# One kernel of cross attention and feed-forward: y's rows and integers in buffers of their own, half a landing buffer for the context, batch 0's K and the last tile's h by quarters

## The reference, cut to what matters

```python
def dyn_quant(x):                       # per row
    s = max(max(|x|) / 127, 1e-8);  return clip(round(x / s), -127, 127), s

x_n   = layernorm(x)
q     = w8a8(x_n, wq, bq)               # integers of x_n times integers of wq, times both scales
k, v  = ctx @ wk.T + bk, ctx @ wv.T + bv            # full precision
p     = softmax(q k^T / sqrt(32) + mask)            # 16 heads, 112 x 375
x     = x + w8a8(p v, wo, bo)
x_n   = layernorm(x)
h     = gelu(int8_matmul(rowwise(x_n), W1) + B1)    # W1, W2: one scale for the whole matrix
x     = x + int8_matmul(rowwise(h), W2) + B2
```

## Time and profile before

| | us |
|---|---|
| median of three executions | 663.83 |
| the three | 659.75, 665.29, 663.83 |
| the profiled execution | 658.58 |
| its span (first to last instruction) | 656.4 |
| PE busy | 638.5 (97%) |
| DVE busy | 474.1 (72%) |
| ACT busy | 461.1 (70%) |
| POOL busy | 223.6 (34%) |
| granted PE clock | 1.00 |

### The profile page before, as it was taken

One profiled execution on the slowest core, in us unless ns is written; L12 is line 12 of the kernel. 1 busy time (PEld: TensorE's weight loads), 2 busy tenths in 40 slices (PEclk: granted clock), 3 DMA queues, 4 the chain that ended last, 5 costly groups with the idle time before them and its releaser, 6 DMA issues.

```text
span 656.4 us, 15000 instructions
## 1 busy us (share of the span) xinstructions
PE 638.5 (97%) x5204; PEld 470.9 (72%) x5204; DVE 474.1 (72%) x1175; ACT 461.1 (70%) x1156; POOL 223.6 (34%) x455
## 2 busy tenths in 40 slices
PE   8898999999999999999999989999999999999999
PEld 4667787777777777768777777877777786767534
DVE  4989788767676766876775834775688768777874
ACT  3545676777887667787687867786777778879702
POOL 3343343252527153530525243341444252321100
DMA  9965865523252443413214253217145231413020
...
DMA packets 80586, 58.68 MB, mean 89 GB/s; under 512 B 57984, under 2 KB 67968, under 8 KB 79872
## 3 DMA queue, kind: packets, MB, share of 16 engines
...
## 4 chain that ended last, share of the span: by engine, by line
PE 75%; DVE 11%; DMA 5%; issue 4%; POOL 3%; ACT 2%; ACTq 0%; DVEq 0%; SPq 0%; POOLq 0%
PE ps_ring L1070 32%; PE ps_t L1104 12%; PE ps_s L1097 7%; PE ps_ring L1176 7%; PE ps_t L1116 6%; PE ps_ring L1189 6%; PE ps_ring L1138 2%; PE ps_ring L1063 1%; DMA w_q<-in_w1T 1%; PE ps_s L1165 1%; DVE cols L843 1%; PE ps_ring L1126 1%; DMA yqT<-o_q 1%; DMA x_in<-in_x 1%; DVE probs L872 1%
## 5 line engine op out<-in xcount | busy, mean ns | idle before, releaser
L872 DVE CUSTOM_DVE_ANT_0 probs<-ps_s,mask_in 112x375 f32<-112x375 f32 x256 | 129.6, 544 | 67.8 <-PE ps_s L1097 54.9
L690 ACT ACTIVATE probs<-probs,neg_max 112x375 f32<-112x375 f32 x256 | 154.5, 607 | 27.1 <-DVE neg_max L872 24.6
L700 ACT ACTIVATE pT<-ps_t 125x336 f32<-125x336 f32 x256 | 109.8, 446 | 70.6 <-PE ps_t L1104 64.7
L1104 PEld LDWEIGHTS ps_t<-ident,probs 112*125 112x125 f32 x768 | 107.9, 188 | 42.3 <-issue 18.6
L1104 PE MATMUL ps_t<-ident,probs 112*125 112x112 f32 x768 | 119.9, 278 | 5.6 <-ACT oT L707 2.4
L609 POOL TENSOR_TENSOR ctx_lo<-ctx_in,ctx_hi 128x376 fp32r<-128x376 f32 x60 | 63.8, 1071 | 124.7 <-ACT ctx_hi L668 124.6
L1070 PE MATMUL ps_ring<-ctx_hi,wk_hi 128*128 128x376 f32 x256 | 90.7, 354 | 1.2 <-DVE wk_lo L765 0.7
L1070 PE MATMUL ps_ring<-ctx_hi,wk_lo 128*128 128x376 f32 x256 | 85.5, 334 | 0.0
L1070 PE MATMUL ps_ring<-ctx_lo,wk_hi 128*128 128x376 f32 x256 | 85.4, 334 | 0.0
L1070 PE MATMUL ps_ring<-wv_hi,ctx_hi 128*125 128x512 f32 x192 | 79.1, 412 | 2.0 <-DVE o L882 1.0
L1070 PE MATMUL ps_ring<-wv_lo,ctx_hi 128*125 128x512 f32 x192 | 75.8, 395 | 0.0
...
## 6 DMA issues: line engine op xcount, KB each, us to landing
...
w_q<-in_w1T SPq DMA_DIRECT2D x2, 1024.0 KB, 11.3
```

The lines of the kernel that those rows point to most:

```text
L690: nc.scalar.activation(probs[:, hd % SP_RING, :], probs[:, hd % SP_RING, :], ACT.Exp, scale=-1.0, bias=neg_max[:, b % 2, hd:hd + 1], accum ...
L700: nc.scalar.activation(pT[0:LR, hd % PT_RING, :], att_bank("T", b, hd)[0:LR, 0:LC * N], ACT.Copy).then_inc(pT_s, 1)
L872: nc.vector.tensor_tensor_reduce(out=probs[:, hd % SP_RING, :], in0=ps_s[hd % HG][0:N, 0:L], in1=mask_in[:, b % 2, :], scale=-1.0, scalar= ...
L1104: last = nc.tensor.transpose(bank[0:LR, lc * N:(lc + 1) * N], probs[:, hd % SP_RING, lc * LR:(lc + 1) * LR], ident[0:N, 0:N])
```

## The change

Seven things, in the words of the code:

1. `yn` and `y_q` are buffers of their own beside `o` and `o_q`. `gather`'s row on DVE waits for `o_quant` of the tile before instead of `y_quant`; `o_quant` and `y_quant` wait each for their own transpose of the tile before.
2. `ctx_in` has two blocks instead of four and one semaphore; each half load waits until the half before it is split on both engines.
3. All `ctx_lo` subtractions are DVE's; POOL's are gone.
4. Batch 0's K goes by quarters of the contraction (`k0` units, `k_first`): a quarter adds its three products to all four K blocks, which stand in the four banks `ps_s`, and waits only for its half of wk and its block of context.
5. The last tile's h is quantised by quarters of 512 columns: DVE takes 0, 1 and 2, ACT takes 3. PE transposes each quarter into a bank of `ps_s` or `ps_t`, DVE copies 0 and 2, ACT 3 and 1, and `down` takes the quarters in the order 0, 3, 1, 2, each as it comes.
6. 13 `warm` units stand at the start, 19 at the end, and none after the last `down`.
7. All five tables of orders are new.

The diff, without the tables, without the new semaphores' declarations and without most unchanged lines:

```diff
-             if use[0] in ("w_T", "so", "w_max", "q", "k", "v", "gather", "o_T", "out_proj", "y_T", "up", "h_T") or use[0] == "down" and use[2] == 0]
+             if use[0] in ("w_T", "so", "w_max", "q", "k", "v", "gather", "o_T", "out_proj", "y_T", "up") or use[0] == "down" and use[2] == 0]
...
-        ctx_in = sb("ctx_in", [P, KC, LP])
+        ctx_in = sb("ctx_in", [P, KC // 2, LP])
...
-        o = yn = sb("o", [P, C])
-        o_q = sb("o_q", [P, C], BF16)
+        o, yn = sb("o", [P, C]), sb("yn", [P, C])
+        o_q, y_q = sb("o_q", [P, C], BF16), sb("y_q", [P, C], BF16)
...
-                sp.dma_start(yqT[:, :, :], o_q[:], transpose=True).then_inc(yqT_s, 16)
+                sp.dma_start(yqT[:, :, :], y_q[:], transpose=True).then_inc(yqT_s, 16)
...
-            def split_lo(b, i):
-                if b == 1 and i == 0:
-                    pool.wait_ge(ctx_lo_s, 4)
-                pool.wait_ge(ctx_hi_s, 4 * b + i + 1)
-                wait_for(pool, k_pe, 4 * (b - 1))
-                wait_for(pool, v_pe, 3 * (b - 1))
-                nc.gpsimd.tensor_tensor(ctx_lo[:, b % 2, i, :], ctx_in[:, i, :], ctx_hi[:, b % 2, i, :].bitcast(FP32),
-                                        ALU.subtract).then_inc(ctx_lo_s, 1)
...
-                act.wait_ge(ctx_in_s[i // 2], 16 * (b + 1))
+                act.wait_ge(ctx_in_s, 16 * (2 * b + i // 2 + 1))
...
-                nc.scalar.activation(ctx_hi[:, b % 2, i, :], ctx_in[:, i, :], ACT.Copy).then_inc(ctx_hi_s, 1)
+                nc.scalar.activation(ctx_hi[:, b % 2, i, :], ctx_in[:, i % 2, :], ACT.Copy).then_inc(ctx_hi_s, 1)
...
-                nc.scalar.activation(k_sb[:, b % 2, g, :], bank_of("k", b, g)[:, 0:LP], ACT.Identity,
+                bank = ps_s[g] if b == 0 else bank_of("k", b, g)
+                nc.scalar.activation(k_sb[:, b % 2, g, :], bank[:, 0:LP], ACT.Identity,
...
-                rows = h[:, F // 2:F]
+                first = 3 * C if t == LAST else F // 2
+                rows = h[:, first:F]
...
-                nc.scalar.activation(h_q[:, F // 2:F], rows, ACT.Identity, bias=round_down[:]).then_inc(h_quant_s, 1)
+                nc.scalar.activation(h_q[:, first:F], rows, ACT.Identity, bias=round_down[:]).then_inc(h_quant_s, 1)
+                if t == LAST:
+                    act.wait_ge(down_pe, t)
+                    for bank, j, count in ((ps_s[2], 3, 4), (ps_s[3], 1, 5)):
+                        act.wait_ge(last_T, count)
+                        nc.scalar.activation(hT[:, 4 * j:4 * j + 4, :].rearrange("p k n -> p (k n)"), bank[:, 0:C // 2].bitcast(BF16), ACT.Copy
+                                             ).then_inc(hT_act, 1)
...
-                act.dma_start(ctx_in[:, 2 * i:2 * i + 2, 0:L], ctxT[b, 2 * i * P:2 * (i + 1) * P, :].rearrange("(k p) l -> p k l", p=P)
-                             ).then_inc(ctx_in_s[i], 16)
+                act.dma_start(ctx_in[:, :, 0:L], ctxT[b, 2 * i * P:2 * (i + 1) * P, :].rearrange("(k p) l -> p k l", p=P)
+                              ).then_inc(ctx_in_s, 16)
...
-                if b >= 1:
-                    act.wait_ge(ctx_lo_s, 4 * (b - 1) + 2 * i + 2)
-                    act.wait_ge(ctx_hi_s, 4 * (b - 1) + 2 * i + 2)
+                wait_for(act, ctx_lo_s, 4 * b + 2 * i)
+                wait_for(act, ctx_hi_s, 4 * b + 2 * i)
...
-                wait_for(dve, y_quant_s, t)
+                wait_for(dve, o_quant_s, t)
...
-                wait_for(dve, yqT_s, 16 * b)
+                wait_for(dve, oqT_s, 16 * b)
...
-                dve.wait_ge(o_quant_s, b + 1)
+                wait_for(dve, y_quant_s, b)
...
-                if b == LAST:
-                    dve.wait_ge(last_T, 1)
-                else:
-                    dve.wait_ge(oqT_s, 16 * (b + 1))
-                round_rows(b, yn[:], y_r, o_q[:], y_round, y_quant_s, y_r_s)
+                wait_for(dve, yqT_s, 16 * b)
+                round_rows(b, yn[:], y_r, y_q[:], y_round, y_quant_s, y_r_s)
...
-                dve.wait_ge(last_T, {"o_T": 1, "y_T": 2, "h_T": 3 + i}[name])
+                dve.wait_ge(last_T, {"o_T": 1, "y_T": 2}[name])
...
-                wait_for(dve, down_pe, t)
-                last_evac(hT[:, 8 * i:8 * i + 8, :], "h_T", i, 8, hT_last)
+                if i == 0:
+                    wait_for(dve, down_pe, t)
+                    dve.wait_ge(last_T, 3)
+                    nc.vector.tensor_copy(hT[:, 0:4, :].rearrange("p k n -> p (k n)"), ps_s[1][:, 0:C // 2].bitcast(BF16)).then_inc(hT_dve, 1)
+                    h_quarter(2)
+                else:
+                    dve.wait_ge(last_T, 6)
+                    nc.vector.tensor_copy(hT[:, 8:12, :].rearrange("p k n -> p (k n)"), ps_t[0][:, 0:C // 2].bitcast(BF16)).then_inc(hT_dve, 1)
...
-                dve.wait_ge(ctx_hi_s, i + 1)
-                nc.vector.tensor_tensor(ctx_lo[:, 0, i, :], ctx_in[:, i, :], ctx_hi[:, 0, i, :].bitcast(FP32), ALU.subtract
+                dve.wait_ge(ctx_hi_s, 4 * b + i + 1)
+                wait_for(dve, k_pe, 4 * (b - 1))
+                wait_for(dve, v_pe, 3 * (b - 1))
+                nc.vector.tensor_tensor(ctx_lo[:, b % 2, i, :], ctx_in[:, i % 2, :], ctx_hi[:, b % 2, i, :].bitcast(FP32), ALU.subtract
...
-                round_rows(b, h[:, 0:F // 2], h_r, h_q[:, 0:F // 2], h_round_lo, h_quant_lo, h_r_s)
+                if b == LAST:
+                    dve.wait_ge(h_r_s, b + 1)
+                    h_quarter(0)
+                    h_quarter(1)
+                else:
+                    round_rows(b, h[:, 0:F // 2], h_r, h_q[:, 0:F // 2], h_round_lo, h_quant_lo, h_r_s)
+            def h_quarter(j):
+                part = slice(j * C, (j + 1) * C)
+                nc.vector.tensor_scalar(h[:, part], h[:, part], h_r, ROUND, ALU.mult, ALU.add).then_inc(h_round_lo, 1)
+                dve.wait_ge(h_round_lo, LAST + 1 + j)
+                nc.vector.tensor_scalar(h_q[:, part], h[:, part], -ROUND, None, ALU.add).then_inc(h_quant_lo, 1)
...
-                if b == 0:
-                    pe.wait_ge(w_lo, 2)
...
+            def k_first(b, k):
+                pe.wait_ge(w_lo, k // 2 + 1)
+                pe.wait_ge(ctx_lo_s, k + 1)
+                for g in range(KC):
+                    cols = slice(g * P, (g + 1) * P)
+                    for t, (w, c) in enumerate(((wk_hi, ctx_hi), (wk_hi, ctx_lo), (wk_lo, ctx_hi))):
+                        last = nc.tensor.matmul(ps_s[g][:, 0:LP], w[:, k, cols], c[:, 0, k, :],
+                                                start=(k == 0 and t == 0), stop=(k == KC - 1 and t == 2))
+                    if k == KC - 1:
+                        last.then_inc(k_pe, 1)
...
-                pe.wait_ge(k_s, 4 * b + g + 1)
+                pe.wait_ge(k_s, 4 * b + g + 1 if b else KC)
...
-                rows_T("y_T", i, o_q, KC, 0)
+                rows_T("y_T", i, y_q, KC, 0)
+            def quarter_T(bank, j):
+                for n in range(4):
+                    k = 4 * j + n
+                    last = nc.tensor.transpose(bank[:, n * P // 2:(n + 1) * P // 2].bitcast(BF16), h_q[:, k * P:(k + 1) * P], ident_bf[:])
+                last.then_inc(last_T, 1)
...
-                pe.wait_ge((h_quant_lo, h_quant_s)[i], t + 1)
-                rows_T("h_T", i, h_q, 8, 8 * i)
+                if i == 0:
+                    pe.wait_ge(masked, 16 * B)
+                    pe.wait_ge(h_quant_lo, LAST + 1)
+                    quarter_T(ps_s[1], 0)
+                    pe.wait_ge(h_quant_s, LAST + 1)
+                    quarter_T(ps_s[2], 3)
+                    pe.wait_ge(h_quant_lo, LAST + 2)
+                    quarter_T(ps_s[3], 1)
+                else:
+                    pe.wait_ge(oT_s, 4 * OT_DONE[B])
+                    pe.wait_ge(h_quant_lo, LAST + 3)
+                    quarter_T(ps_t[0], 2)
...
-                    nc.tensor.matmul(ps_s[0][:, :], ident_bf[:], warm_row, start=True, stop=True)
+                    nc.tensor.matmul((ps_t, ps_s)[n][0][:, :], ident_bf[:], warm_row, start=True, stop=True)
...
+                quarter = i
+                if b == LAST:
+                    quarter = (0, 3, 1, 2)[i]
+                    pe.wait_ge(*((hT_dve, 1), (hT_act, 1), (hT_act, 2), (hT_dve, 2))[i])
+                elif i == 0:
+                    pe.wait_ge(hT_s, 32 * (b + 1))
...
-                    if b == LAST:
-                        pe.wait_ge(hT_last, 2)
-                    else:
-                        pe.wait_ge(hT_s, 32 * (b + 1))
...
-                    k = 4 * i + n
-                    last = nc.tensor.matmul(bank, hT[:, k, :], w2_q[:, k, :], start=(k == 0), stop=(k == FK - 1))
+                    k = 4 * quarter + n
+                    last = nc.tensor.matmul(bank, hT[:, k, :], w2_q[:, k, :], start=(i == 0 and n == 0), stop=(i == 3 and n == 3))
...
-            units = {"w_T": w_T, "so": so, "w_max": w_max_unit, "q": q, "k": k_unit, "v": v_unit, "S": S, "T": T, "PV": PV, "gather": gather,
```

(19 more changed lines are left out.)

286 lines of the change are left out of this document (138 added, 148 removed).

## The result

The changed kernel took **670.84 us** (median of six executions, 669.87 to 682.21), the kernel before 661.53 us beside it: a ratio of **1.0162** (95% interval 1.0134 to 1.0190), and 1.0171 (1.0113 to 1.0228) when it was run again on another chip. The execution of 682.21 us ran in a slower state of the chip and is left out of the ratio. The forecast was 660.0 us, no change; it is slower by 1.6%, at the very edge of the range of 651 to 671, and the sign is the one that had a chance of 0.22.

What follows compares the result with a forecast made beforehand. It took TensorE (PE), busy for 638.5 of 656.4 us, as the bound. Start 0, middle +0.9 and tail -1.3 and -1.5 gave -1.9, so 661.86 - 1.9 = 660.0 us, range 651 to 671.

Steps and rivals of the forecast that it cites:

- sign that the prediction gave for being right: First scores near 42.93 us; at most two ACT context waits over 2 us; last `down` 6.3 us after the reciprocal.
- sign of being wrong: First scores over 4 us earlier or later, or DVE becoming the engine that PE waits for.
- the start: Up to the first score rows: earlier K against later context landings, taken as even, 0 us, range -3 to +5.
- Middle: The 540 us between the ends: one more late landing +1.9, y's buffers -1.0, together +0.9 us, range -5 to +8.
- the +1.9 of the prediction: Half landing buffer in the middle: one more late context load makes PE wait, +1.9 us, range -1.9 to +8.
- Own buffers: Middle: y's own buffers free the gather and quantising rows from waits, -1.0 us, gain between 0 and 2.0.
- Splits on DVE: Context subtractions moved from POOL to DVE: 30.2 us more DVE work after 60 us, covered by PE, 0 us.
- Tail: From the last reciprocal to the span's end: quarters -1.3 us, no fillers behind the last `down` -1.5 us.
- Rival C: Slower: landing buffer shows, six late halves at 1.9 us in ACT's order, +5 at the start; +13.6, 675.5 us, chance 0.22.

Runs made afterwards that it cites:

- experiment 8: The changed kernel with only SP's order mended, two W2 loads and the move of batch 1's row sums ahead of scale transfers; ratio to the kernel before 1.0061.
- experiment 9: The changed kernel with SP's order mended and the full landing buffer, y's rows sharing o's buffer; ratio to the kernel before 0.9996.
- experiment 5: The changed kernel with the full landing buffer again, loads one place ahead, y's rows sharing o's buffer; ratio to the kernel before 1.0078.
- experiment 6: The changed kernel with the context subtractions of batches 1 to 15 back on POOL; ratio to the kernel before 1.0294.
- experiment 1: The kernel before with the tail alone changed: last h by quarters, no filler behind the last `down` nor the one ahead of it; ratio 0.9997.

## Why the prediction was wrong

Nearly every sign that the prediction gave for being right came true: first scores at 44.70 (within 2 us of 42.93), one wait of ACT for the context of over 2 us behind 60 us (4.34; a second was 1.86), 6.2 us from the reciprocal to the last `down`. One sign of being wrong showed: PE's largest waits are for DVE's rows (6.6 us for score rows, 3.5 for `o`), though DVE was late because it waited for transfers, not because it was busy. No sign looked at the stretch between the first scores and the second `gather`, where most of the loss is.

**The step that failed: nothing was reckoned for the stretch from 60 us to the second `gather`, and 0 for the start.** At 60 us, where the prediction ends its start, PE has been idle for 2.8 us more than before (50.82 us busy for 53.59), the clock of 0.94 has cost some 3.5, and 1.8 us of fillers are gone: about **+4.5** by this estimate, near the upper end of +5. The first scores hide it, since V 1.0, w_T 0.5 and 0.6 and two filler units stand ahead of them before and behind them now. The landing of batch 1's first half was seen as a danger (11.3 us) and weighed as even with the gains; it took 9.4 us with ACT, DVE and PE behind it. From 60 us to the second `gather` another 10.3 us are lost (14.8 less 4.5), where the prediction's middle has +0.9 for its whole length. SP's queue was not walked through: I wrote of ACT's order and the fillers, and never asked what stands ahead of the W2 loads. Experiments 8 and 9 give those places 1.0% and 0.8% of the time, experiment 5 gives the full landing buffer 0.8%. The two add up: 1.0162 less 0.0084 (experiment 5) less 0.0101 (experiment 8) is 0.998, and both together measured 0.9996.

**The clock was no term at all.** Over its compared executions the changed kernel's mean granted clock is 0.9886, before's 0.9976 to 0.9985; 0.9 to 1.0% of 669 us is some 6 of the 10 us. Four of seven waits of PE of 1.8 us or more had a fall behind them that cost 1.7 us again, and every wait was priced at its own length alone.

**Middle: predicted +0.9, measured +5.7 between the first and the last `gather`,** of which 2.5 + 1.9 + 1.0 us of waits and 1.7 of clock fall in the first 27 us; the first two waits are those behind the late row sums. Behind the second `gather` the middle is right: 474.8 us to the last one for 475.2 before, -0.4. There the half buffer costs 2.6 to 2.9 us in single profiles (471.9 us in experiment 5, 472.2 in experiment 9), near the +1.9 of the prediction, with two late landings of 6.2 us on ACT; the new orders give about as much back. That they do was not in the prediction, so the -0.4 is in part luck.

**Own buffers: -1.0 predicted.** Wrong in its reason for the rows, since DVE's own order already does what the buffer would; not measured alone, since the kernel before has no room for them.

**Splits on DVE: 0 predicted.** +0.4% alone, needed beside the half buffer (experiment 6). DVE was busy for 492 us (predicted 505), POOL 165.6 (160): cover was there, as said. The rule of the Trainium skill that a DVE instruction with two SBUF inputs and a GpSimd instruction that reads SBUF contend (SBUF — State Buffer, "Who interferes with whom") hardly shows as a cost in the changed kernel: DVE's 64 splits took 570 ns on average against 540, and one alone took over 1.3 us (2155 ns).

**Tail: -2.8 predicted,** -2.6 in the two parts named (6.2 us from the reciprocal where 6.3 was said, 3.4 from there to the end), -1.6 for the stretch, since gather to reciprocal took 1.0 us longer, and next to nothing in the time (experiment 1).

**Rival C** had the right sign and a size near the measured one (+13.6 us, for 9 between the medians and 12.8 between the spans), by half of the right mechanism: not six late halves in the middle but one at the start and two behind, and a queue that it did not name. That the sizes are near is luck. The Trainium skill (DMA: Bandwidth & Descriptors, "Rules for kernel authors") advises to issue early and wait late; this case agrees, with 9.4 us between issue and landing for a load that ACT waited for at once.
